# Graph transformer layer on one core: the two score column addresses of an edge block move from TensorE's registers to a ring that SyncE fills

## The reference, cut to what matters

```
score = a_s[:, src] + a_d[:, dst] + aw_e[:, None]*elem + ab[:, None]   # 4 heads x 100,000 edges
w = exp(-relu(score / 20))
pooled[src] += w * feats[dst];  row_sum[src] += w;  out = pooled / row_sum
```

## Time and profile before

| | |
|---|---|
| timed, median of 3 (lowest to highest) | 3498.57 us (3489.51 to 3504.27) |
| profiled execution: span from first to last instruction | 3482.0 us |
| profiled execution: what lies around the span | not given with the profile |
| stretch with graph items on TensorE | 1712 to 3056 us, 1344 us |
| TensorE matmul busy in the span | 3221.5 us (93%) |
| granted TensorE clock, mean over the span | 0.967 |

### The profile page before, as it was taken

One profiled execution on the slowest core, in us unless ns is written; L12 is line 12 of the kernel. 1 busy time (PEld: TensorE's weight loads), 2 busy tenths in 40 slices (PEclk: granted clock), 3 DMA queues, 4 the chain that ended last, 5 costly groups with the idle time before them and its releaser, 6 DMA issues.

```text
span 3482.0 us, 43961 instructions
## 1 busy us (share of the span) xinstructions
PE 3221.5 (93%) x13869; PEld 2325.5 (67%) x13869; DVE 2347.5 (67%) x6155; ACT 1184.5 (34%) x2126; POOL 2056.9 (59%) x1776
## 2 busy tenths in 40 slices
PE   8888999999899999999889899898999998999989
PEld 6665667777677777767566666576666666665668
DVE  7998888854454555545677777676666666769951
ACT  3443333333233333323333334243342424422320
POOL 3330577777777777777377677773777777711100
PEclk9999999999999999999999999899999999999999
DMA  3422122222322222322355454454455555422125
GB/s 115 144 96 78 37 50 44 49 49 43 81 47 47 49 50 44 76 55 58 101 136 141 130 138 136 125 141 138 134 152 143 147 147 146 132 82 71 69 101 174
DMA packets 226182, 339.26 MB, mean 97 GB/s; under 512 B 51501, under 2 KB 179755, under 8 KB 225702
## 3 DMA queue, kind: packets, MB, share of 16 engines
q0 software_dynamic: 67840, 119.33, 16.2%
q1 hardware_dynamic: 119502, 162.08, 14.4%
q10 hardware_dynamic: 38616, 55.04, 5.0%
HBM read 248.16 MB, written 87.29 MB: 96 GB/s over the span
## 4 chain that ended last, share of the span: by engine, by line
PE 63%; DVE 21%; issue 5%; another core or an unknown queue 5%; POOL 2%; ACT 2%; DMA 1%; DVEq 1%; ACTq 0%; SPq 0%
PE bank_v L1817 16%; PE bank_a L1804 16%; PE bank_e L1859 8%; PE bank_v L1749 4%; PE bank_a L1721 3%; PE bank_v L1792 3%; PE bank_a L1643 3%; PE bank_v L1709 3%; PE bank_v L1967 2%; POOL arena L804 2%; DVE acc L1503 1%; DVE st L1080 1%; DVEq L1511 1%; DVE arena L1243 1%
## 5 line engine op out<-in xcount | busy, mean ns | idle before, releaser
L804 POOL DMA_INDIRECT arena<-gather_table,arena x880 | 954.7, 1085 | 456.2 <-issue 247.4
L846 POOL DMA_INDIRECT edge_records<-acc x800 | 969.3, 1212 | 402.9 <-issue 402.9
L1817 PE MATMUL bank_v<-W_sb,gT 128*125 128x256 f32 x3200 | 747.1, 385 | 18.3 <-issue 13.7
L1804 PE MATMUL bank_a<-hT,W_sb 128*128 128x500 f32 (+1 forms) x1664 | 716.1, 578 | 13.8 <-issue 12.3
L1817 PEld LDWEIGHTS bank_v<-W_sb,gT 128*125 128x125 f32 x3200 | 602.7, 191 | 122.0 <-issue 26.1
L1804 PEld LDWEIGHTS bank_a<-hT,W_sb 128*128 128x128 f32 x1664 | 317.4, 194 | 326.2 <-issue 307.2
L1859 PE MATMUL bank_e<-arena 128*125 128x260 f32 x1760 | 467.9, 410 | 5.6 <-issue 3.1
L881 ACT ACTIVATE gT<-bank_a,cols 128x500 f32<-128x500 f32 (+1 forms) x416 | 274.2, 661 | 466.1 <-PE bank_a L1804 375.1
L1859 PEld LDWEIGHTS bank_e<-arena 128*125 128x125 f32 x1760 | 327.5, 197 | 57.8 <-issue 7.7
L881 ACT ACTIVATE hT<-bank_a,cols 128x500 f32<-128x500 f32 (+1 forms) x208 | 145.6, 747 | 491.5 <-PE bank_a L1643 378.2
L1239 DVE TENSOR_TENSOR arena<-arena 128x1024 f32<-128x1024 f32 x220 | 268.3, 1220 | 0.0
(11 more groups left out here) (292 smaller groups left out, 4366.1 us busy)
## 6 DMA issues: line engine op xcount, KB each, us to landing
residual<-xs SPq DMA_DIRECT2D x60, 500.0 KB
xs<-residual SPq DMA_DIRECT2D x58, 500.0 KB
arena<-edge_rows ACTq DMA_DIRECT2D x220, 125.0 KB
queries<-qT_out SPq DMA_DIRECT2D x48, 500.0 KB
qT_in<-queries ACTq DMA_DIRECT2D x39, 500.0 KB
arena<-gather_table,arena POOLq DMA_INDIRECT x880
edge_records<-acc POOLq DMA_INDIRECT x800
slice_weights<-arena SPq DMA_DIRECT2D x12, 1000.0 KB, 5.0
```

Of the source, the lines that this page charges most:

```text
L804: e.indirect_dma_start(g_of(j)[:, i, :], None, table_d, bass.IndirectOffsetOnAxis(ap=node[:, TE * j + i:TE * j + i + 1].bitcast(I32), axis ...
L846: e.indirect_dma_start(rec_d, bass.IndirectOffsetOnAxis(ap=pos_i[:, f:f + 1], axis=0), r3[:, f, :], None).then_inc(d_rec, 16)
L1804: o = e.matmul(b[:, 0:n], W[:, k, f * P:(f + 1) * P], hv[:, k, 0:n], start=k == 0, stop=k == KC - 1)
L1817: o = e.matmul(b[0:R, i % 2 * D:(i % 2 + 1) * D], gv[:, f, i * R:(i + 1) * R], W2_sb[:, f * D:(f + 1) * D], start=f == 0, stop=f == FB - 1)
```

## The change

SyncE gets a part in `("edge", k)`: it loads the column addresses of block k+3 (of blocks 0 to 3 at k = 0) into its own registers and copies the 12 columns of each half block, 128 partitions of 24 bytes, from `as3` to a new ring `as_ring` of six blocks by a DMA. From block 6 on it first waits for `e_full[0]`, as ScalarE does. TensorE waits for these copies (`as_in`, one semaphore for each place of the ring) as a fourth wait of the item, reads the ring at fixed addresses and loads no registers.

```
+        as_ring = sb("as_ring", [P, 6 * 2 * 3 * HG], BF16)
+        d_asin = [sem(f"d_asin{i}") for i in range(NR)]
+        as_of = lambda j, h: as_ring[:, (j % NR * 2 + h) * 3 * HG:(j % NR * 2 + h + 1) * 3 * HG]
+        as_in = lambda j: (d_asin[j % NR], 32 * (j // NR + 1))
 # SyncE
+                elif stage == "edge":
+                    k, = at
+                    if k == 0:
+                        e.wait_ge(as_set, 1)
+                        e.wait_ge(d_tidload, 16)
+                    for j in (range(4) if k == 0 else range(k + 3, min(k + 4, NB))):
+                        if j >= NR:
+                            e.wait_ge(e_full[0], j - 5)
+                        for h in range(2):
+                            col = e.value_load(tids[0:1, NH + 2 * j + h:NH + 2 * j + h + 1], min_val=0,
+                                               max_val=(NT - 1) * 3 * HG)
+                            e.dma_start(as_of(j, h), as3[:, bass.ds(col, 3 * HG)]).then_inc(as_in(j)[0], 16)
 # TensorE
                         e.wait_ge(*rows_in(j))
+                        e.wait_ge(*as_in(j))
                         for i in range(TE):
                             o = e.matmul(ps_as[...], ohT_ring[...],
-                                         as3[:, bass.ds(col_at[i // TH], 3 * HG)], start=True, stop=True)
+                                         as_of(j, i // TH), start=True, stop=True)
...
-                    if 1 <= k <= NB:
-                        col_at = [e.value_load(tids[0:1, NH + i:NH + i + 1], min_val=0, max_val=(NT - 1) * 3 * HG)
-                                  for i in (2 * (k - 1), 2 * (k - 1) + 1)]
```

## The result

The kernel after took 3519.11 us, the median of 4 runs (3511.58 to 3528.81), against 3498.58 us of 4 runs before: ratio 1.0062, 95% interval [1.0036, 1.0087]. It is slower by some 20 us, where 3489 us was forecast. The profiled execution has a span of 3509.8 us, 27.8 more than before.

A forecast was written before the change was run, and what follows sets the result against it. TensorE was taken to bound the stretch with graph items, with 137.1 us of holes. The removal's 9 us, with SyncE's wait and the copies at 0, took 3498.6 to 3489.6, say 3489 us; range 3455 to 3518.

The forecast's parts named there:

- The loads on TensorE's sequencer: Holes right behind the sums (L1859): removing 440 register loads saves 9 us, bounds 0 and 10.9.
- The address arithmetic: Before the score matmuls (L1848): each of 45 waits ends 0.1 us sooner, 4.5 us, bounds 1.8 and 5.9.
- The sum of the removal, 9 us: TensorE, loads and address arithmetic together: of 13.5 us two thirds kept, 9 us, the rest lost to waiting for VectorE.
- SyncE's part: SyncE's added loads, copy issues of 0.25 us and new wait: 1.7 us per block fits; wait priced at 0, bounds 0 and 30.
- The DMA engines: 440 added copies, 16 to 144 packets of 69 ns each: 5 points on a DMA share of 49, bounds 2 to 20.
- What would feel it are the gathers ... So 0.: Copies' load on the DMA engines: VectorE waited only 3.2 us for gathers, so the cost was put at 0.
- VectorE's lateness. Most of the 77.7 us is TensorE waiting for a sum: Waits before the score matmuls: mostly for VectorE's sum, not removed; a TensorE that comes sooner waits longer.
- the copies crowd the gathers: Rival at GpSimd, 87% occupied: copies slow each gather by 0.14 us, net +26 us, 3524 us; chance 0.15.
- Nothing moves: Rival: TensorE's loads were already hidden and savings return as waiting for VectorE, 0 to 3 us, 3498 us; chance 0.20.

The follow-up runs named there:

- e2: Kernel before without TensorE's register loads, score matmuls reading as3 at a fixed address, no copies: ratio 0.9980 to the kernel before.
- e7: Kernel before with TensorE's two register loads moved half an item later, no copies: ratio 0.9997 to the kernel before.
- e5: As e3, but each of the 440 copies moves 24 bytes of one partition instead of 128: ratio 1.0068 to the kernel before.
- e3: Changed kernel, but SyncE copies from a fixed address and loads no registers: ratio 1.0036 to the kernel before.
- e11: Kernel before with GpSimd's gathers for the first six blocks only: 3320.45 us, ratio 0.9503 to the kernel before.
- e8: As e3, but ScalarE issues the 440 copies instead of SyncE: ratio 1.0043 to the kernel before.
- e18: As e3, but the copies read the row numbers in DRAM and nobody reads the ring: ratio 1.0003 to the kernel before, on a fast chip.
- e17: Changed kernel, but ScalarE itself copies the columns by activation, no DMA added: ratio 1.0001 to the kernel before, on a fast chip.
- e19: Changed kernel run once more, unchanged, on another fast chip: 3383.74 us, ratio 0.9989 to the kernel before.

## Why the prediction was wrong, step by step

- **The loads on TensorE's sequencer**: right on the holes, which went from 10.9 to 3.5 us (e2: 6.9 in 6). That each us of them is a us of the kernel is not borne out: e7 closes them as well and gains nothing.
- **The address arithmetic**: right. In every item in which TensorE waited for VectorE's first sum it started 0.14 us behind it before and 0.06 after: 0.08 us, where 0.1 was taken.
- **The sum of the removal, 9 us**: the size fits. e2 measured 0.9980 [0.9962, 0.9998], 7 us with 1 to 13 possible; at the fast places the whole change, copies included, 0.9989 [0.9978, 1.0000], 0 to 7 us.
- **SyncE's part**: its issues were mis-sized, 0.49 us at the median for 0.25 taken, but the wait never mattered: from the end of the second copy's issue to its score matmul there are 5.4 us at the least and 28.6 at the median. No wait of TensorE is put down to the copies.
- **The DMA engines**: 144 packets a copy, the dear end of the count, but 9 ns each and not 69. The share in the stretch rose from 0.49 to 0.52, less than the 5 points taken, and e5 costs no less with hardly any of the pieces. What the prediction took from the Trainium skill's row on 512 bytes ("DMA: Bandwidth & Descriptors", table at the head), that pieces of 24 bytes would be dear, the trace does not bear out: 9 ns a packet. The mean gather went from 1087 to 1098 ns.
- **"What would feel it are the gathers ... So 0."** This step failed: the copies, put at 0, cost 0.0056, 20 us (e3 against e2), over twice what the removal gains. It asked only who waits for data. VectorE waited no longer for gathers (0.2 us after, 3.2 before); TensorE waited longer for VectorE, and more of TensorE's signals to VectorE were late. No row of mine showed such signals, because of this step:
- **"VectorE's lateness. Most of the 77.7 us is TensorE waiting for a sum"**: misread. VectorE was late because it had itself stood 120.4 + 31.0 us at "remote" waits, and these are TensorE's own signals on their way. The waiting runs in a circle, TensorE to VectorE and back, so a late signal comes back as idle time of TensorE; how much of each lateness does is not shown. e11 shows that 100 of 138 us of idle time go with the gathers (their data traffic goes with them, so it isn't said which part of a gather does it).
- **The rivals**: "the copies crowd the gathers" had the side and nearly the size (3524), by a mechanism that did not occur: the gathers stayed at 1.10 us, not 1.3, so the nearness is luck. "Nothing moves" describes the fast places, which no run before the change had shown.

What stays open: why the signals are late at some places and not at others (chips 9, 6 and 5 against 15 and 8; the traces have the same work and the same gather durations, and each chip served one batch or two, so it may be the time or what else ran on the machine, and not the chip); whether a copy's issue or its 16 landings does the harm (a copy without landings was not tried); how the copies lengthen the stage in e8, in which no more signals are late than without them; whether a source in SBUF matters (e18 fell on a place where nothing costs); and whether e17 keeps the 7 us where signals are late. No version was measurably faster than the kernel before with all of its work in it.

## What to carry to other kernels

When TensorE waits for another engine, read that engine's own waits before calling it late; if these are "remote" waits for TensorE, look when its signal came: here the signal was late and not VectorE, and removing work from TensorE's sequencer left that as it was (share late 40% before, 38% in e2). Beside a stream of gathers, hundreds of added small transfers can cost more than their bytes, their lead times or the DMA share say: here 440 of them cost 20 us with every copy over 5 us early. And time a change of half a per cent at more than one place: here it is a loss at one and no loss at the other. One profile of each kernel is not enough for idle times of this size either.

## What the hardware showed that was not expected

- The same program takes 3384 and 3386 us on two chips and 3495 to 3515 us on three, 3.2 to 3.9% more (two batches on one of these differ by 20 us). The difference lies in the stage with gathers: 1269.9 us in e19, 1393.4 in the kernel after. Of these 123.5 us, 84 are idle time of TensorE; for the rest the same matmuls are under way longer, 1222 against 1182 us, at a granted clock of 0.94 against 0.97 (1712 to 2900). What lowers the clock is not shown.
- TensorE's signal reached VectorE up to 13.29 us after the modelled end of its matmul before the change, and within 0.46 us (0.04 at the median) on the fast chips. VectorE's and ScalarE's signals were within 0.02 us in both.
- At the fast places another bound shows: VectorE waits 111.9 us for gathers (3.2 us in the earlier trace rows).
- A copy of one partition's 24 bytes took longer to issue (705 ns) than one of 128 such pieces (602 ns), and its data went in pieces of 2 bytes.
- With the address in a register the issue was shorter, 493 ns at the median, and the same, 494 ns, on a fast chip (e19).
